# Second products of a gated MLP: three of eight go into the sums by accumulating DMAs

## The reference, cut to what matters

```python
def dequantize(imatrix, scales, zeros, group_size, out_dtype):
    rs = jnp.repeat(scales, group_size, axis=0)
    rz = jnp.repeat(zeros, group_size, axis=0)
    return ((imatrix.astype(rs.dtype) - rz.astype(rs.dtype)) * rs).astype(out_dtype)
...
gate = jax.nn.silu(jnp.dot(x, gate_proj))
up = jnp.dot(x, up_proj)
return jnp.dot(gate * up, down_proj)
...
x = x + jnp.tanh(g_xattn[0]) * xattn(layernorm(x), ctx, ...)
x = x + jnp.tanh(g_ffn[0]) * ffn(layernorm(x), ...)
```

## Time and profile before

| what | us |
|---|---|
| median of 3 runs | 1664.07 (1658.07 to 1664.68) |
| profiled execution, its own time | 1667.74 |
| its span | 1665.9 |
| TensorE matmuls busy | 1574.3 (95%) |
| TensorE weight loads busy | 805.3 (48%) |
| VectorE busy | 1517.5 (91%) |
| GpSimd busy | 1452.7 (87%) |
| ScalarE busy | 990.1 (59%) |

### The profile page before, as it was taken

One profiled execution on the slowest core, in us unless ns is written; L12 is line 12 of the kernel. 1 busy time (PEld: TensorE's weight loads), 2 busy tenths in 40 slices (PEclk: granted clock), 3 DMA queues, 4 the chain that ended last, 5 costly groups with the idle time before them and its releaser, 6 DMA issues.

```text
span 1665.9 us, 40474 instructions
## 1 busy us (share of the span) xinstructions
PE 1574.3 (95%) x16614; PEld 805.3 (48%) x16614; DVE 1517.5 (91%) x1483; ACT 990.1 (59%) x1133; POOL 1452.7 (87%) x891
## 2 busy tenths in 40 slices
PE   6898999897889999999999999999999999999996
PEld 3566667575533444444444444444444444444444
DVE  5687878776689999999999999999999999999997
ACT  4677778676445555555555555555555555555552
POOL 4576777676688999999999999999999999999975
PEclk9899999999899999999999999999999999999999
DMA  5655666655332222222222222222222222222128
GB/s 123 162 142 141 169 150 149 150 142 136 104 105 64 76 76 77 76 77 76 77 76 77 76 75 78 74 76 70 75 75 76 77 76 77 76 76 76 39 101 303
DMA packets 169522, 166.66 MB, mean 100 GB/s; under 512 B 11918, under 2 KB 135502, under 8 KB 169322
## 3 DMA queue, kind: packets, MB, share of 16 engines
q1 hardware_dynamic: 168186, 163.74, 34.9%
q10 hardware_dynamic: 1152, 0.33, 0.1%
HBM read 113.92 MB, written 16.78 MB: 78 GB/s over the span
## 4 chain that ended last, share of the span: by engine, by line
PE 84%; issue 5%; POOL 4%; DVE 3%; DMA 1%; ACT 1%; SPq 1%; ACTq 0%; DVEq 0%; POOLq 0%
PE bank L1168 63%; PE bank L1077 4%; PE bank L1066 3%; PE bank L1109 2%; POOL oacc L602 2%; DVE acc L950 2%; PE bank L1029 2%; PE bank L1040 2%; PE bank L1025 2%; PE bank L1033 2%; PE bank L1087 1%; PE bank L1056 1%; PE bank L1037 1%; PE bank L1045 1%; POOL raw_z L541 1%
## 5 line engine op out<-in xcount | busy, mean ns | idle before, releaser
L950 DVE SCALAR_TENSOR_TENSOR acc<-bank,scale,acc 128x1024 f32<-128x1024 f32 x784 | 950.5, 1272 | 13.7 <-PE bank L1168 8.9
L1168 PE MATMUL bank<-xT,w_int 128*128 128x512 f16 x3584 | 847.9, 380 | 13.2 <-ACT d_part L787 5.2
L602 POOL TENSOR_TENSOR oacc<-oacc,d_part 128x1024 f32<-128x1024 f32 x335 | 792.6, 2366 | 34.3 <-ACT d_part L787 19.1
L787 ACT ACTIVATE d_part<-bank,scale 128x1024 f32<-128x1024 f32 x335 | 372.7, 1113 | 379.9 <-PE bank L1168 373.3
L1168 PEld LDWEIGHTS bank<-xT,w_int 128*128 128x128 f16 x3584 | 349.5, 98 | 439.7 <-DVE acc L950 8.5
L1168 PE MATMUL bank<-h_hi,d_int 128*128 128x512 f16 x896 | 340.2, 380 | 9.0 <-ACT acc L767 2.5
L1168 PE MATMUL bank<-h_lo,d_int 128*128 128x512 f16 x896 | 339.5, 379 | 0.0
L541 POOL TENSOR_TENSOR raw_z<-raw_w,raw_z 128x512 int32<-128x512 int32 x168 | 264.1, 1573 | 9.0 <-DMA raw_z<-in_L_ffn_gate_z_dram 5.3
L1168 PEld LDWEIGHTS bank<-h_hi,d_int 128*128 128x128 f16 x896 | 87.4, 98 | 148.4 <-DVE acc L950 26.2
L974 DVE SCALAR_TENSOR_TENSOR oacc<-bank,scale,oacc 128x1024 f32<-128x1024 f32 x113 | 143.8, 1273 | 0.8 <-PE bank L1168 0.8
L668 ACT ACTIVATE pT<-bank 96x1024 f16<-96x1024 f16 x128 | 123.6, 1018 | 34.2 <-PE bank L1077 33.8
(11 more groups left out here) (84 smaller groups left out, 1377.2 us busy)
## 6 DMA issues: line engine op xcount, KB each, us to landing
raw_w<-in_L_ffn_gate_w_dram SPq DMA_DIRECT2D x56, 256.0 KB, 3.0
raw_z<-in_L_ffn_gate_z_dram SPq DMA_DIRECT2D x56, 256.0 KB, 3.7
raw_w<-in_L_ffn_up_w_dram SPq DMA_DIRECT2D x56, 256.0 KB, 3.0
raw_z<-in_L_ffn_up_z_dram SPq DMA_DIRECT2D x56, 256.0 KB, 3.7
raw_w<-in_L_ffn_down_w_dram SPq DMA_DIRECT2D x56, 256.0 KB, 2.7
raw_z<-in_L_ffn_down_z_dram SPq DMA_DIRECT2D x56, 256.0 KB, 3.4
vt<-vn_hl SPq DMA_DIRECT2D x64, 192.0 KB
vt<-vn_hl SPq DMA_DIRECT2D x64, 160.0 KB
```

Of the source, the lines that this page charges most:

```text
L602: nc.gpsimd.tensor_tensor(into, into, part, ALU.add).then_inc(d_added, 1)
L787: nc.scalar.activation(d_part[:, (count(c, x, False) - 1) % 2, :], pair[slot][:, :, :].rearrange("p h r -> p (h r)"), ACT.Copy, scale=scal ...
L950: nc.vector.scalar_tensor_tensor(out=into, in0=pair[u % 4][:, :, :].rearrange("p h r -> p (h r)"), scalar=scale[:, par, i, m, k:k + 1], in ...
L1168: last = nc.tensor.matmul(dst[:, h, :], weights, rows_of(h, part), start=(part == 0), stop=(part == 1))
```

## The change

At the place 2 the second product is no longer VectorE's. VectorE keeps place 7. GpSimd adds those of the places 1, 2, 4 and 6. Those of the places 0, 3 and 5 are scaled by ScalarE into one of two new buffers `d_more`, and then a DMA issued from GpSimd's queue adds the buffer to `oacc` (source and target in SBUF, 128 x 1024 fp32, 512 KB). There is a semaphore for each of the two buffers. ScalarE waits for the landing of the DMA two before when it reuses a `d_more` buffer. Every taker now waits for the earlier sum of the same part of `oacc`, by whatever engine or DMA it was made. The eleven late products keep their takers. Over the kernel 54 products leave VectorE, 164 go by DMA, and GpSimd makes 225 adds in place of 335.

```diff
-    D_DVE = (2, 7)
+    D_DVE, D_DMA = (7,), (0, 3, 5)
...
+        d_more = sb("d_more", [P, 2, TB], fp32)
...
+        d_landed = [sem("even_d_landed"), sem("odd_d_landed")]
...
-        def count(c, x, mine):
-            own = [r for r in range(NK) if by_dve(r) == mine]
-            late = [r for r in range(FIRST_LATE, x + 1) if (r in LATE_DVE) == mine] if c == NC - 1 else []
+        def taker(c, x):
+
+            if c == NC - 1 and x >= FIRST_LATE:
+                return "dve" if x in LATE_DVE else "pool"
+            at = (x + LAG) % NK
+            return "dve" if at in D_DVE else "dma" if at in D_DMA else "pool"
+
+        def count(c, x, *takers):
+
+            own = [r for r in range(NK) if taker(0, r) in takers]
+            late = [r for r in range(FIRST_LATE, x + 1) if taker(c, r) in takers] if c == NC - 1 else []
...
+        def scaled(c, x):
+            return count(c, x, "pool", "dma")
+
+        def landed(n):
+            return d_landed[(n - 1) % 2], 16 * ((n - 1) // 2 + 1)
+
+        def added(c, x):
+
+            by = taker(c, x)
+            n = count(c, x, by)
+            return (d_summed, n) if by == "dve" else (d_added, n) if by == "pool" else landed(n)
...
         def down_emptied(c, x):
-            return (d_summed if by_dve(x) else d_scaled), count(c, x, by_dve(x))
+            return (d_summed, count(c, x, "dve")) if taker(c, x) == "dve" else (d_scaled, scaled(c, x))
...
             def add_down(c, x):
-                n = count(c, x, False)
-                pool.wait_ge(d_scaled, n)
-                if n > 1:
-                    pool.wait_ge(d_added, n - 1)
+                pool.wait_ge(d_scaled, scaled(c, x))
+                n = count(c, x, taker(c, x))
+                if n == 1:
+                    pool.wait_ge(oacc_zeroed, NCT)
+                if ahead(c, x)[0] >= 0:
+                    pool.wait_ge(*added(*ahead(c, x)))
+                into = oacc[:, x % NCT, x // NCT // SC % NT, :]
+                if taker(c, x) == "pool":
+                    nc.gpsimd.tensor_tensor(into, into, d_part[:, (n - 1) % 2, :], ALU.add).then_inc(d_added, 1)
                 else:
...
+                    nc.gpsimd.dma_start(into, d_more[:, (n - 1) % 2, :], accum_op=ALU.add).then_inc(landed(n)[0], 16)
...
             def scale_down(c, x, par, slot):
-                n = count(c, x, False)
+                n = count(c, x, taker(c, x))
                 act.wait_ge(down_ready, c * NQT * NCT + x + 1)
-                if not isinstance(n, int) or n > 2:
-                    act.wait_ge(d_added, n - 2)
-                nc.scalar.activation(d_part[:, (count(c, x, False) - 1) % 2, :],
+                if taker(c, x) == "pool":
+                    if n > 2:
+                        act.wait_ge(d_added, n - 2)
+                    part = d_part[:, (n - 1) % 2, :]
+                else:
+                    if n > 2:
+                        act.wait_ge(*landed(n - 2))
+                    part = d_more[:, (n - 1) % 2, :]
+                nc.scalar.activation(part,
                                      pair[slot][:, :, :].rearrange("p h r -> p (h r)"), ACT.Copy,
...
             def add_down(c, x, par, slot):
-                n = count(c, x, True)
+                n = count(c, x, "dve")
                 dve.wait_ge(down_ready, c * NQT * NCT + x + 1)
-                if n > 1:
-                    dve.wait_ge(d_summed, n - 1)
-                else:
+                if n == 1:
                     dve.wait_ge(oacc_zeroed, NCT)
-                cc, xx = ahead(c, x)
-                if cc >= 0 and not taken_by_dve(cc, xx):
-                    dve.wait_ge(d_added, count(cc, xx, False))
+                if ahead(c, x)[0] >= 0:
+                    dve.wait_ge(*added(*ahead(c, x)))
...
-                    pe.wait_ge(d_added, count(NC - 1, x, False))
+                    pe.wait_ge(d_added, count(NC - 1, x, "pool"))
+                    for n in range(2):
+                        pe.wait_ge(*landed(count(NC - 1, x, "dma") - n))
```

More of the change, by code:

```diff
@@ L624, in one @@
                     x = down_unit(c, u)
-                    if u % 3 == 2 and x is not None and not by_dve(x):
+                    if u % 3 == 2 and x is not None and taker(c, x) != "dve":
                         add_down(c, x)
@@ L1000, in one @@
                     x = down_unit(c, u)
-                    if u % 3 == 2 and x is not None and by_dve(x):
+                    if u % 3 == 2 and x is not None and taker(c, x) == "dve":
                         add_down(c, x, par if x >= 0 else 1 - par, u % 4)
@@ L1206, in turn_col @@
                 x = NQT * NCT - NCT + ct_
-                pe.wait_ge(d_summed if x in LATE_DVE else d_added, count(NC - 1, x, x in LATE_DVE))
+                pe.wait_ge(*added(NC - 1, x))
                 for b in range(TT):
```

17 lines of the change are left out of this document (3 added, 14 removed).

## The result

| | before | after |
|---|---|---|
| median of 4 runs each, us | 1663.97 (1658.07 to 1664.68) | 1636.47 (1635.00 to 1637.04) |
| profiled execution, own time, us | 1667.74 | 1636.69 |
| its span, us | 1665.9 | 1634.9 |

The changed kernel is faster: ratio 0.9839, interval 0.9820 to 0.9858, 27.5 us by the medians. The forecast was 1648, a gain of 16 to 18 us. The time lies under the low end of its range, 1640.

A forecast was written before the change was run, and what follows sets the result against it. The prediction took VectorE's place 2 to stall TensorE in the steady part: 41.8 quarters x 0.35 = 14.6 us, plus 3.4 outside, together 18 us. That gave 1649.7 or 1646.1 by baseline; it said 1648, range 1640 to 1735.

The forecast's parts named there:

- The bound and the cause of the steady part: 700 to 1580 us: a quarter (96 matmuls) takes 21.07 us, TensorE alone 20.72; VectorE's place 2 makes the stall.
- VectorE: Steady quarters: VectorE's 21.03 us busy, less one L974 of 1.27, gives 19.76 us, 0.96 under TensorE's 20.72.
- the pair at the quarter's end: VectorE's L974 and L957, 1.27 + 1.97 us, 0.5 too much for two TensorE steps; stall taken as 0.
- The issue on GpSimd, d: GpSimd's queue: each DMA issue takes 1.37 us, the middle of 0.37 and 2.37, giving GpSimd 20.2 us a quarter.
- rival 1: GpSimd's in-order queue becomes the bound, losing from d = 1.67 us; 1718 at 2.0, 1777 at 2.37; chance 0.24.
- Rival 1's second form: VectorE shuts GpSimd out while it writes descriptors; one issue hit a quarter, up to 1.97 us: 59 us, 1723.
- The cover of h_lo: GpSimd's order: h_lo ends at 7.5 us of the quarter, place 3's product begins at 9.5: 2 us of cover.
- Landing: Accumulating DMAs land in 6 us, bounds 3.8 and 14.8; some 8.3 us are left before a buffer is reused.
- the upper of the two figures: DMA share in the steady part: added traffic adds 0.22, or 0.43 if reading the target doubles it, to 0.25.
- Rival 2's example: DMA buffers: landing over about 9.3 us costs 81 us per us more; at 11 us about 1770; chance 0.10.
- the sum, in its term for the start-up: Twelve places 2 outside 700 to 1580 us, start-up's included, priced at one stall of 0.28 us each: 3.4 us.

The follow-up runs named there:

- e1: Against the changed kernel, VectorE keeps place 2 as well as 7, the three DMAs stay: median 1650.71 us, ratio 0.9934 to before.
- e11: Against the changed kernel, VectorE's one product is place 2 instead of 7, GpSimd takes 7: 1657.17 us, ratio 0.9943 to before.
- e4: Against the kernel before, ScalarE writes the first product of each of the sixteen sums, no memsets: 1661.26 us, ratio 0.9971.
- e2: Against the changed kernel, two DMAs a quarter (places 2 and 5), GpSimd adds five: 1642.51 us, ratio 0.9893 to before.
- e7: Against the changed kernel, ScalarE writes the first product of each sum, no memsets: 1632.93 us, ratio 0.9834 to before.
- e10: Changed kernel with ScalarE writing the first product of each sum, no memsets, run once more: 1633.95 us, ratio 0.9841 to before.
- e6: Against the changed kernel, each accumulating DMA is cut into four of 256 columns, twelve issues a quarter: 1944.4 us, ratio 1.1705 to before.

## Why the prediction came out as it did

**The bound and the cause of the steady part: right, with one thing left out.** TensorE's pace of 20.72 us a quarter, the 0.35 us above it, and place 2 of VectorE as the cause stood as read. Measured: 20.72 and 0.34. e1 and e11 show the cause by keeping it. Left out was that VectorE's 21.03 us a quarter were over 20.72 already, so that before the change its load alone would have held TensorE up by 0.31 us. e1 and e11 tell place from load: with 20.70 and 19.4 us of VectorE a quarter, both under 20.72, place 2 still cost 0.28 and 0.29 us. e4 shows the load: VectorE is full and a quarter takes 21.20. Taking place 2 away removed both at once.

**VectorE: right.** 19.76 us a quarter were forecast, 844.55 / 880 x 20.72 = 19.9 measured. That the two agree so well is partly luck: L981 took 0.53 us less than counted, and the adds more, since they now follow TensorE's pace (seven in 9.05 us below, ten in 12.12 in the earlier trace rows). Place 2 is now passed without a break, and the pair at the quarter's end, which I put at 0.5 us too much for two steps, costs TensorE nothing. VectorE's timeline after:

```profile
1018.34 1.28 DVE L995 SCALAR_TENSOR_TENSOR oacc<-bank,scale,oacc 128x1024 f32<-128x1024 f32 x1
1019.53 1.44 DVE L981 SCALAR_TENSOR_TENSOR acc<-acc 128x1024 f32<-128x1024 f32 x1
1021.13 9.05 DVE L974 SCALAR_TENSOR_TENSOR acc<-bank,scale,acc 128x1024 f32<-128x1024 f32 x7 [0.16 <-PE bank L1189]
```

The pair was even shorter than I counted, L981 1.44 us instead of 1.97, so VectorE is through early enough to wait 0.16 us for TensorE.

**The issue on GpSimd, d: size off, on the safe side.** I took 1.37 us of bounds 0.37 to 2.37; it is 0.944. GpSimd has 17.56 us a quarter and not 20.2. Of the 2.6 us between them d explains 1.3; the rest is that the instruction behind an issue starts before the issue ends, and that the three subtractions of a quarter took 1.333 us each in place of 1.608. That sank rival 1, to which I had given 0.24. The Trainium skill (DMA: Bandwidth & Descriptors, section Latency and other measured facts) has about 1 us until a GpSimd DMA's first byte, and an estimate by it gave 19.1 us a quarter. With 0.944 us an issue, the trace is nearer to that than to my middle, though the page's figure is not the time for which the queue is held.

**Rival 1's second form, VectorE shutting the issues out: no sign of it.** GpSimd's timeline after has the three issues of a quarter:

```profile
1009.92 1.05 POOL L620 DMA_DIRECT2D oacc<-d_more  x1
...
1014.65 0.85 POOL L620 DMA_DIRECT2D oacc<-d_more  x1
...
1021.96 0.88 POOL L620 DMA_DIRECT2D oacc<-d_more  x1 [2.08 <-ACT d_more L811]
1022.70 2.32 POOL L606 TENSOR_TENSOR h_lo<-acc,h_hi 128x1024 f16<-128x1024 f32 x1
```

All of them run beside VectorE's adds of first products and take about the same; over the steady part they last 0.848 to 1.492 us with the middle one at 0.884. The rule of the Trainium skill weighed there (SBUF — State Buffer, section Who interferes with whom) would leave the issues alone beside adds with an input in PSUM; the trace agrees, but holds no case in which it would not. The two-input L981 never stood beside an issue in it, so whether that would hold one up stays open.

**The cover of h_lo: right.** The issue of place 0 starts late because GpSimd waits 2.08 us for ScalarE's d_more, and h_lo stands behind it, as the working had it. h_lo ends at 1025.02. TensorE's timeline after, where the product of place 3 first reads it:

```profile
1027.19 0.38 PE L1189 MATMUL bank<-h_lo,d_int 128*128 128x512 f16 x1
```

That leaves 2.17 us, against the 2 forecast.

**Landing: right.** 5.0 us (4.5 to 10.0) against the 6 taken. Of the 164 landings all but one are under the 8.3 us that were left, and ScalarE's d_more waits for TensorE alone. The DMA share rose by 0.44, the upper of the two figures. (Rival 2's example was summed too low: 1.7 us over 9.3 at 81 us each are 138 us, which gives about 1784 from 1646, not 1770.)

**The step that failed is the sum, in its term for the start-up.** It priced the twelve places 2 outside 700 to 1580 us "by the one stall, 0.28 us: 3.4 us". Ten of them brought that alone: six belong to the 48 steady quarters (2.0 us at 0.34), four to the last 132.8 us, which gained 1.4. The other two are in the start-up, priced at 0.56 us, and that gained 7.8. The working read only rows of the steady part and of the end, and took the cause found there for the cause everywhere. The start-up had another bound, GpSimd (48.19 us of work against 41.4 of TensorE's), and there the half of the change that I weighed only for whether GpSimd stayed under TensorE was a gain: two adds of 2.37 us a quarter less for three issues of 0.944, 4.7 us against 2.8. e1 shows it (all of the start-up's gain without VectorE's half), e2 shows a part of it, and e4, e7 and e10 show that relieving GpSimd in the start-up by another way shortens it too. About 1.6 of the 7.8 us are the clock's lower level behind one of the waits, which one trace of before shows; whether it falls there in every execution wasn't looked for. For a gain of that kind there was no rival, so the range ended 8 us under the forecast.

Of the 11.5 us between the forecast, 1648, and the median, 1636.5, the start-up is 7.2. Another 1.9 come from setting the forecast between 1646.1 (from the median) and 1649.7 (from a profiled execution that was slower than the median), and 1.9 are what no stretch accounts for.

**What stays open.** The traces place 25.6 us, the medians differ by 27.5. The stretch ahead of the MLP varies by more than the 1.9 us between them. What makes it vary was not looked for.

## What to carry to other kernels

Price a change by stage: a stage whose engine has extra work (clearing of sums, first loads) can be bound by another engine than the steady part: here two quarters of 56 gave 7.8 of the 25.6 us. Where units pass through a ring of buffers, look for the place at which an instruction is wedged in, not for the engine's share: at 92% busy it was late, at 96% not. And before an add is moved to an accumulating DMA, compare the issue's length with the add's. Cutting the same bytes into four pieces cost 308 us here (e6 against the change, by the medians).
